# Waiting for the addition that empties a score bank, or for the maximum taken behind it

## The reference, cut to what matters

```
pooled = masked softmax pooling of x over each sequence
c_kv = pooled @ W_kv_down;   k, v, q (16 heads of 8), rotary parts of 32
scores = q.k per head + (q_rope.k_rope), the same for all heads
scores = scores / sqrt(8 + 32);  causal mask;  w = softmax(scores)
x  = x + (w @ v) @ W_o
c2 = x @ W[category of the sequence] + b[category]
weights cw = 8 best of 64 experts inside the 4 best of 8 groups, from sigmoid(c2 @ gate_w.T)
y  = sum over experts of cw * ((silu(c2 @ wg) * (c2 @ wu)) @ wd), plus one shared expert
x  = x + y
```

## Time and profile before

| | before |
|---|---|
| median of 3 runs | 741.04 us (739.32 to 742.67) |
| the profiled execution | 741.32 us |
| its span, from the first to the last instruction | 739.5 us |
| mean granted TensorE clock | 0.989 of full speed |
| PE busy | 709.9 us, 96% of the span |
| VectorE busy | 547.2 us, 74% |
| ScalarE busy | 444.7 us, 60% |
| GpSimd busy | 425.2 us, 57% |

### The profile page before, as it was taken

How to read it: one execution, slowest core, us unless ns; L and a number is a source line. 1 busy time by engine, 2 the same in 40 slices (tenths; PEclk the granted TensorE clock), 3 DMA queues, 4 the chain that set the end, 5 groups by cost and what they waited for, 6 DMA issues and landing times.

```text
span 739.5 us, 15765 instructions
## 1 busy us (share of the span) xinstructions
PE 709.9 (96%) x5628; PEld 547.5 (74%) x5628; DVE 547.2 (74%) x1144; ACT 444.7 (60%) x857; POOL 425.2 (57%) x352
## 2 busy tenths in 40 slices
PE   8878899999999999999999999999999999999997
PEld 7756676677877778777787777777787777877885
DVE  5766659886598676887688865987768876886664
ACT  3865766568455765568555684557654685555553
POOL 2644488665466644556455654666455564666665
PEclk9998999999999999999999999999999999999999
DMA  8453542445433434434454463434535345444451
GB/s 279 143 199 90 148 108 82 130 106 157 103 123 111 140 110 116 143 96 143 109 120 132 108 154 104 121 108 137 119 115 140 100 142 117 101 123 147 129 134 44
DMA packets 66750, 93.00 MB, mean 126 GB/s; under 512 B 7760, under 2 KB 26640, under 8 KB 66672
## 3 DMA queue, kind: packets, MB, share of 16 engines
q1 hardware_dynamic: 62784, 88.07, 43.4%
q10 hardware_dynamic: 3888, 3.93, 1.5%
HBM read 88.37 MB, written 3.15 MB: 124 GB/s over the span
## 4 chain that ended last, share of the span: by engine, by line
PE 72%; DVE 11%; ACT 9%; issue 3%; POOL 2%; DMA 2%; SPq 1%; POOLq 0%; ACTq 0%; DVEq 0%
PE banks L979 70%; DVE act_w L946 3%; DVE hid L958 2%; ACT s_t L402 2%; ACT hid_hi L535 2%; POOL hid_lo L633 2%; ACT banks L523 1%; ACT L523 1%; ACT L402 1%; PE banks L1059 1%; SPq L269 1%; DMA k_rope<-rope_sum 1%; DVE head_max L704 1%; DVE s_t L703 1%; ACT v_blk L389 1%
## 5 line engine op out<-in xcount | busy, mean ns | idle before, releaser
L633 POOL TENSOR_TENSOR hid_lo<-hid,hid_hi 128x512 fp32r<-128x512 f32 (+1 forms) x264 | 341.9, 1295 | 275.4 <-ACT hid_hi L535 270.3
L946 DVE TENSOR_TENSOR act_w<-banks,cwb 128x512 f32<-128x512 f32 x254 | 174.6, 687 | 126.6 <-ACT banks L523 123.5
L523 ACT ACTIVATE banks<-banks 128x512 f32<-128x512 f32 x254 | 147.2, 582 | 141.3 <-PE banks L979 138.9
L535 ACT CAST hid_hi<-hid 128x512 fp32r<-128x512 f32 (+1 forms) x264 | 162.7, 616 | 76.8 <-DVE hid L958 75.1
L958 DVE TENSOR_TENSOR hid<-act_w,banks 128x512 f32<-128x512 f32 (+1 forms) x264 | 181.3, 687 | 24.8 <-PE banks L979 2.7
L979 PE MATMUL banks<-c_hi,wg_hi 128*128 128x512 f32 x264 | 119.2, 452 | 4.2 <-DVE act_w L946 4.2
L979 PE MATMUL banks<-hid_hi,wd_hi 128*128 128x512 f32 (+1 forms) x264 | 107.1, 406 | 4.7 <-POOL hid_lo L633 4.4
L979 PE MATMUL banks<-hid_hi,wd_lo 128*128 128x512 f32 (+1 forms) x264 | 104.0, 394 | 0.0
L979 PE MATMUL banks<-hid_lo,wd_hi 128*128 128x512 f32 (+1 forms) x264 | 104.0, 394 | 0.0
L979 PE MATMUL banks<-c_lo,wg_hi 128*128 128x512 f32 x264 | 103.9, 394 | 0.0
L979 PE MATMUL banks<-c_hi,wg_lo 128*128 128x512 f32 x264 | 103.9, 394 | 0.0
(11 more groups left out here) (158 smaller groups left out, 805.7 us busy)
## 6 DMA issues: line engine op xcount, KB each, us to landing
cwb<-cw_scratch SPq DMA_DIRECT2D x254, 256.0 KB, 3.7
k_blk<-in_cond_w SPq DMA_DIRECT2D x112, 64.0 KB
xf<-in_x_feat SPq DMA_DIRECT2D x8, 256.0 KB, 4.1
out_feat<-y ACTq DMA_DIRECT2D x8, 256.0 KB, 3.4
wg_raw<-in_we_gate SPq DMA_DIRECT2D x7, 256.0 KB, 5.5
wu_raw<-in_we_up SPq DMA_DIRECT2D x7, 256.0 KB, 5.8
wd_raw<-in_we_down SPq DMA_DIRECT2D x7, 256.0 KB, 5.9
xf<-in_x_tok SPq DMA_DIRECT2D x6, 256.0 KB, 2.8
```

Of the source, the lines that this page charges most:

```text
L523: nc.scalar.activation(dst, gate_bank(p)[:, :], ACT.Silu).then_inc(S["silu_done"], 1)
L535: nc.scalar.copy(hid_hi[0:n, p % NH, :], hid[0:n, p % NH, :]).then_inc(S["hi_ready"], 1)
L633: nc.gpsimd.tensor_sub(hid_lo[0:n, p % NH, :], hid[0:n, p % NH, :], hid_hi[0:n, p % NH, :].bitcast(F32)).then_inc(S["lo_ready"], 1)
L946: nc.vector.tensor_mul(act_w[:, p % NH, :], gate, weight)\
```

## The change

The addition now counts up a semaphore of its own, `score_read`. VectorE's maximum waits for that count instead of `dve_chain`, so `CHAIN` goes from 25 to 21. Three waits of TensorE for `biased_tile` become waits for `score_read`; the last one also asks for three tiles, not four (A2 holds tiles 0 and 2). GpSimd's subtraction and all else still wait for `biased_tile`.

```diff
-        CHAIN = 25
+        CHAIN = 21
...
-                    chain(nc.vector.tensor_add(s, ps, bias), blk)
+                    nc.vector.tensor_add(s, ps, bias).then_inc(S["score_read"], 1)
+                    dve.wait_ge(S["score_read"], blk * TILES + t + 1)
                     nc.vector.tensor_reduce(head_max[:, t, :], s_t[:, t, :].rearrange("p (n k) -> p n k", k=SEQ), AX, ALU.max)\
                         .then_inc(S["biased_tile"], 1)
...
                     else:
-                        pe.wait_ge(S["biased_tile"], blk * NG + 2)
+                        pe.wait_ge(S["score_read"], blk * NG + 2)
...
                     else:
-                        pe.wait_ge(S["biased_tile"], blk * TILES + TILES)
+                        pe.wait_ge(S["score_read"], blk * TILES + TILES)
...
                     if p == LENT:
                         if following is not None:
-                            pe.wait_ge(S["biased_tile"], following * TILES + TILES)
+                            pe.wait_ge(S["score_read"], following * TILES + TILES - 1)
```

More of the change, by code:

```diff
@@ L185, in adaln_attention_moe @@
                 q_ps rope_ps k_ps k_again_ps q_ready rot_ready rope_summed k_ready v_ps v_ready rope_score_ps rope_mask_ready
-                score_tile_ps biased_tile sub_tile prob_tile probT_ps probT_ready av_ps att_ready attT_ps attT_ready
+                score_tile_ps score_read biased_tile sub_tile prob_tile probT_ps probT_ready av_ps att_ready attT_ps attT_ready
                 wo_ps x2_ready c2tok_ps c2tok_ready c2_ps c2_ready gate_ps tanh_gate score_ready biased_ready cw_ready cwT_ps cwT_ready
```

## The result

| | before | after |
|---|---|---|
| median of the runs of this comparison | 741.81 us (6 runs) | 735.84 us (6 runs) |
| ratio | | 0.9938, 95% interval 0.9919 to 0.9957 |
| the profiled execution, its span | 741.32, 739.5 us | 735.65, 733.9 us |
| PE busy | 709.9 us, 96% | 708.6 us, 97% |

The change makes the kernel faster by 0.62%, with an interval of 0.43 to 0.81%. Of 741.8 us that is 4.6 us (3.2 to 6.0). The two medians of this comparison lie 6.0 us apart, at the upper end of that interval. Measured again beside other runs of the kernel before, the medians were 740.4 and 735.52 us, 4.9 apart, and the ratio 0.9937 (4.7 us); so the text goes by the ratios.

A forecast was written before the change was run, and what follows sets the result against it. TensorE, busy 709.9 of 739.5 us, was taken to bound the kernel. Six waits (3.5 us) plus block 1 (0.35) give 3.85 us off the 741.04 us median: 737.2 us, range 733.8 to 740.3.

The forecast's parts named there:

- VectorE and the two other waits: nothing: VectorE's changed counts, and TensorE's waits at the transposes and the up product of unit 6: no gain or cost.
- Six waits disappear whole: 3.5 us: TensorE's second round of scores, blocks 2 to 7: wait over 0.15 us before needed, 0.59 us each, 3.5 us.
- The part that passes: Blocks 2 to 7: of 0.59 us saved at each second round, about 0.57 reaches the end.
- The path to the exponentials, with no room: ScalarE's SiLU, rounding and table load behind the second round: VectorE's `hid` just allows 0.57 us earlier, zero margin.
- the table load: Sign on ScalarE, line 402: some 1.1 us behind unit 5's SiLU as now; 1.5 would mean the hand-back.
- The wait for `hid_lo`: Sign on TensorE at unit 6's down product: the wait stays 0.45 us, both sides moving by 0.57 to 0.58.
- Block 1: 0.35 us: Block 1's second round restarts 0.71 us sooner; at half clock that is worth 0.35 us.
- the case in which TensorE's clock falls and rises at the same instants: Block 1, clock changes at unchanged times: gain 0.35 us; the other cases gave 0.71 or 3.8 us.
- my first rival: Block 1's shorter gap keeps TensorE's clock up or restores it sooner: 735.5 to 734.0 us; chance 0.33.
- Rival 2, the hand-back: Before the exponentials, unit 4's rounding follows VectorE, not TensorE: gain only 1.1 us, 739.9 us; chance 0.17.
- Rival 3: Routing weights (`cwb` loads) land late for units 7 and 8: slower, 745.5 us at 10 us landings; chance 0.05.

The follow-up runs named there:

- The longer wait: Changed kernel with the second round in blocks 2 to 7 also waiting for act_w of unit 3 on VectorE: 744.21 us, ratio 1.0069.

## Why the prediction was right

It said 737.2 us, a gain of 3.85, with a range of 733.8 to 740.3; measured were 735.84 us and, by the ratio, a gain of 4.6 us (3.2 to 6.0). The mechanism was the one foretold, and one term was too small.

- *VectorE and the two other waits: nothing.* Right, by the kernel with only these (1.0006, 0.9993 to 1.0019).
- *Six waits disappear whole: 3.5 us.* Right. The distance of 0.91 us has become 0.33, and block 1's old wait with the new ones in blocks 2 to 7 gains 3.4 us. The part that passes was foretold at 0.57 us per block and was 0.55 in the mean. The gain of a period swings between 0.42 and 0.66 us: it is 0.42 to 0.52 in the periods that begin with the second round of blocks 2, 4 and 6, and 0.65 to 0.66 in those of blocks 3 and 5. Part of that, 0.08 us, is the next point.
- *The path to the exponentials, with no room.* Right, and tighter than I said in half of the blocks: in blocks 3, 5 and 7 the table load stands 1.12 to 1.14 us behind the SiLU, not 1.5; in blocks 2, 4 and 6 the rounding comes only when VectorE's `hid` is there, and the table load 1.20 to 1.21 us behind the SiLU, so some 0.08 us is handed back. The wait for `hid_lo` is still 0.46 us in block 7 and 4.4 us in all. The longer wait shows the same from the other side.
- *Block 1: 0.35 us.* This is the term that was mis-sized. The wait itself shrank as said (2.53 to 1.84 us). I took the case in which TensorE's clock falls and rises at the same instants. One profile of the changed kernel looks like it behind the restart (6.8 us at half clock, 19.35 us against 19.72 to 19.92), but it has no half clock behind the second gap, so over the whole of block 1 it gained as much as the others. In the five profiles with both gaps 3.4 of 10.2 us at half clock are gone and the part is 2.1 us shorter (96.1 against 98.2 in the mean), in a sixth it is 3.7 us shorter; these are near the cases of my first rival. The timed runs show less: 1.3 us between the kernel with block 1's old wait and the changed one (0.9954 against 0.9937, with overlapping intervals), and 0.9 us (a loss of 0.3 to a gain of 2.1) with block 1 alone. So the term is larger than 0.35 us in each of the profiles; the timed runs put it at about 0.9 to 1.3 us and can't by themselves exclude 0.35. With the 3.4 us of blocks 2 to 7 that is 4.3 to 4.7 us, where 4.6 and 4.7 were measured.

That 737.2 us lies only 1.4 us from 735.84 is no proof of the sum. The kernel before had a median of 741.04 us when the forecast was made and 740.4 to 741.8 beside the other kernels, and the largest uncertainty, the clock in block 1, was set at its smallest value.

I had one profile of before and argued from it that the idle time ahead of the fall is the same in both kernels. What failed is to take the instant of the change as a property of the kernel: the clock fell at 64.72, 0.59 us ahead of the restart, in the kernel before, 1.86 us behind the restart in the first profile of the changed kernel and 0.20 us behind it in the second. The Trainium skill, "TensorE: Matmul & The Clock Gate", Part 1, "What's actually happening", said that these instants vary from run to run; this case's traces agree: two profiles of one kernel have 6.8 and 3.4 us at half clock behind restarts after 1.86 and 1.84 us idle. By it the median could gain more than in the case I chose, by up to 1.5 us; the prediction says so and leaves it out of the number.

Rival 2, the hand-back, is refuted by the rows above but for the 0.08 us of blocks 2, 4 and 6. Rival 3 is refuted as well: the one wait for a `cwb` load in the changed kernel (1.0 us) lies in block 1, and no load took more than 6.9 us. The prediction let such a landing eat the whole gain from 9.3 us on; by its own rows that is 9.2 us, from issue to use as it is now.

## What to carry to other kernels

A wait should name the event that frees the resource; where a copy is made first and the rest reads the copy, that is the copy, and the trace shows at once what it is worth: the distance from start to start at a place that doesn't wait, beside the same distance at the place that does. Before adding such gains up, look whether the engine behind follows this one or another. And where TensorE idles for some 2 us, as here, price the half clock behind it too, over several profiles and over a stretch that takes in all such gaps, since one gap of one profile shows only one of the cases. Filling the gap with later work was worth 3.3 us in the kernel before, as much as six of the removed waits, and 1.0 us in the changed one; moving the work that makes the second gap was worth 3.3 us there.

## What the runs showed of the hardware

The same VectorE instruction took twice as long at one place. The multiplication of the pooling weights, both of whose inputs lie in SBUF, took 1.41 us at unit 6 beside a GpSimd subtraction, and 0.69 us where it was moved. First the timelines of VectorE and GpSimd in the changed kernel, then VectorE's in the kernel with the pooling work earlier:

```profile
79.73 1.41 DVE L866 TENSOR_TENSOR pool_p<-pool_p,stats 128x512 f32<-128x512 f32 x1
...
79.33 1.26 POOL L633 TENSOR_TENSOR hid_lo<-hid,hid_hi 128x512 fp32r<-128x512 f32 x1 [3.31 <-ACT hid_hi L535]
```

```profile
74.96 0.69 DVE L866 TENSOR_TENSOR pool_p<-pool_p,stats 128x512 f32<-128x512 f32 x1
```

GpSimd ended at 80.59; from there to the end at 81.14 it is 0.55 us, 0.14 less than the 0.69 us of the instruction when undisturbed, as if the work had begun hardly before. The Trainium skill, "SBUF — State Buffer", section "SBUF: two separate sides", says of a VectorE operation with two SBUF inputs and a GpSimd operation that reads SBUF that they use one port pair in turn, and the later one waits for the whole other instruction. This case's trace agrees but for the 0.14 us: the subtraction had begun 0.40 us earlier (79.33) and took its usual time (1.26 us). The products of lines 947 and 959, which read a bank as one input, took 0.69 us beside the same subtractions. So 0.7 of the 2.65 us of pooling work ahead of unit 9 (78.52 to 81.17) is this; it is one place in one kernel, and no run separates it from the rest of the 3.3 us gained by the move.
